# Three masked attention stages rebuilt around 32-row products shared by four heads

## The chip, the cores and the metric

The kernel runs on one core of one Trainium2 chip. The metric is the device time of one execution, in microseconds. The core has a matmul engine (TensorE, PE in the views; its weight loads are PEld), VectorE (DVE), ScalarE (ACT), GpSimd (POOL) and SyncE (SP), which here only issues transfers. The engines run side by side and meet at semaphores.

## The reference

A decoder of four layers works on x of 8 batches, 256 positions and 128 features. Each layer has attention, a second attention (or something like it) and a feed-forward part. The change touches three attention stages, all with 16 heads of 8 features, all computing, for each batch and head,

```python
h = _layernorm(x)
q, k, v = h @ Wq.T + bq, src @ Wk.T + bk, src @ Wv.T + bv   # split in 16 heads of 8
p = softmax(scale * q @ k.T + mask)
x = x + (p @ v) @ Wo.T + bo
```

L0a (layer 0) takes src = h, a causal mask and weights with a rank-32 correction. L0x (layer 0) takes src = the context and the "trinity" mask: 192 image positions see their own third, 64 text positions see all image positions and earlier text. L2a (layer 2) takes src = h, a causal mask and no bias, and turns q and k by rope tables first.

## The kernel before, in words

Weights stay in SBUF, x too (tile x_resid). A prologue (load_and_turn) loads everything by one SP queue, waits for all of it and transposes it on TensorE. The stages follow one another with a barrier between them: L0a, L0x, the layer-0 experts, L1a, L1x, the experts, L2a, L2x, the experts, L3a, L3x, the experts.

A product of 8 features would use 8 of TensorE's 128 rows. The kernel before (multi_head) uses all 128 rows instead: for each head g, VectorE writes kTm[:, g, :], the keys with the 120 rows of the other heads set to zero (L775), and each product contracts 128 rows. Every batch has these steps:

- turn (L591) transposes h; projections (L514, with a 1-row bias product L516 behind each) make q, k and v. keys_and_values (L770 to L775) copies v and k out and makes the 16 masked copies.
- score(g) (L530, L534): for both halves of the queries, q times masked keys with the queries on PSUM's partitions, and the mask as a bf16 product with an identity. VectorE takes each row's maximum (L807). For the 128 first queries only 128 keys are computed.
- The maxima are transposed (L637), negated and split into two bf16 parts, nm (L812, L813).
- logits(g) (L543, L547, L556): the same products with the keys on the partitions, plus the negated maximum by a selecting product, plus the mask. ScalarE takes exp (L721). weigh(g - LAG) (L582) multiplies the probabilities by v, with a column of ones for the sums: six TensorE instructions per head that load 128 columns of weights and stream 9.
- VectorE divides (L834, L836), TensorE transposes y (L670) and projects it (L514, L516), VectorE adds it to x and takes the statistics (L845, L143 to L147).

The order on each engine is written out by hand. In PE's batch loop all 16 scores come first, then the wait for the maxima, then 16 logits with weigh some heads behind, then the next batch's turn and projections and the end of this batch. An f32 product is two instructions in the trace, each with a weight load of its own and each streaming its columns twice; a bf16 product is one.

## Time and profile before

| what | us |
|---|---|
| median of the 2 runs shown (3786.05 to 3790.34) | 3788.2 |
| span of the profiled execution | 3777.7 |
| L0a, from its first h to L0x's first h | 489.22 |
| L0x, to L0n's first h | 494.07 |
| L2a, to L2x's first h | 490.31 |
| PE busy in the whole span | 3163.1 (84%) |

The profiled execution's own time is its span and what lies around it, about 10.5 us by the median. In the views, a time is from the start of the span, "x2" counts instructions, a bracket at a row's end tells how long the engine was idle before and for whom, and PEclk is the granted clock of TensorE: 1.00 is 2.4 GHz and 0.50 is 1.2 GHz. The start of a matmul row is reliable, its end is modelled, so the pace of a stream is read from the distance between starts.

### The profile page before, as it was taken

To read this page: it belongs to the slowest core of one execution; us is meant where nothing else is said; L and a number is where in the kernel's file an instruction comes from. 1 tells how busy PE (TensorE), PEld (TensorE's weight loads), DVE (VectorE), ACT (ScalarE), POOL (GpSimd) and SP (SyncE) were. 2 spreads that over 40 slices of the span, in tenths; PEclk is the share of its full clock that TensorE was granted. 3 is DMA by queue.
4 is the path that set the end of the run, shared out by engine and by line. 5 is a ranking of instruction groups with operands and counts; after the bars stand their busy time and mean duration, and the time that the engine had idled before them with its cause. 6 is when DMAs were issued, how large, how long until landed. Compare 5 with 4: busy or idle time off the path is not lost. (4 is left out here: it accounts for less than half of the span.)

```text
span 3777.7 us, 55936 instructions
## 1 busy us (share of the span) xinstructions
PE 3163.1 (84%) x19172; PEld 2651.0 (70%) x19172; DVE 1363.3 (36%) x4181; ACT 811.9 (21%) x1508; POOL 67.9 (2%) x136
## 2 busy tenths in 40 slices
PE   5999989999769898965896888884699589898699
PEld 4777767777658787843796777673598367676588
DVE  3323232323242535322221333323333354555344
ACT  1111111111122323322232111112233112121222
POOL 1000000000000000000000000000000000000000
PEclk8887878888889899965898889897799589888699
DMA  3000000000000000000002000000000000000000
GB/s 93 0 0 0 0 1 0 0 0 0 1 1 0 0 0 0 0 0 0 0 0 82 1 0 0 0 1 0 1 0 0 0 9 3 6 3 3 1 0 11
DMA packets 19119, 20.41 MB, mean 5 GB/s; under 512 B 1800, under 2 KB 14320, under 8 KB 19056
## 3 DMA queue, kind: packets, MB, share of 16 engines
q1 hardware_dynamic: 19056, 19.59, 1.6%
q8 instruction: 37, 0.61, 0.1%
q14 instruction: 26, 0.21, 0.0%
HBM read 18.54 MB, written 1.05 MB: 5 GB/s over the span
## 5 line engine op out<-in xcount | busy, mean ns | idle before, releaser
L543 PE MATMUL L3x_bank<-L3x_hT,L3x_kTm 128*128 128x256 f32 x512 | 167.3, 424 | 7.6 <-DVE neg_max L813 7.6
L530 PE MATMUL L2a_bank<-L2a_kTm,L2a_qT 128*128 128x128 f32 (+1 forms) x512 | 127.5, 384 | 35.9 <-DVE L2a_kTm L775 24.9
L543 PE MATMUL L2a_bank<-L2a_qT,L2a_kTm 128*128 128x256 f32 (+1 forms) x512 | 150.2, 378 | 7.6 <-DVE neg_max L813 7.6
L543 PE MATMUL L0a_bank<-L0a_qT,L0a_kTm 128*128 128x256 f32 (+1 forms) x512 | 146.9, 372 | 8.9 <-DVE neg_max L813 8.9
L543 PE MATMUL L0x_bank<-L0x_qT,L0x_kTm 128*128 128x256 f32 (+1 forms) x512 | 146.6, 371 | 8.9 <-DVE neg_max L813 8.9
L721 ACT ACTIVATE L3x_probs<-L3x_msum 128x512 f32<-128x512 f32 x128 | 80.6, 630 | 337.9 <-DVE L3x_msum L821 337.9
L565 PE MATMUL L1a_bank<-L1a_qT,L1a_kTm 128*128 128x256 f32 (+1 forms) x512 | 142.4, 360 | 11.5 <-issue 9.7
L821 DVE TENSOR_TENSOR L3x_msum<-L3x_bank,L3x_mcol 128x512 f32<-128x512 f32 x128 | 88.5, 691 | 158.9 <-PE L3x_bank L547 158.2
L721 ACT ACTIVATE L2a_probs<-L2a_bank 128x384 f32<-128x384 f32 x128 | 62.9, 491 | 382.6 <-PE L2a_bank L556 382.6
L1323 PEld LDWEIGHTS L2f_psY<-scores_L_experts_L,L2f_hidden 128*128 128x128 f32 x1024 | 134.1, 193 | 8.9 <-issue 2.6
L1337 PE MATMUL L2f_psG<-hT,scores_L_experts_L 128*128 x512 | 132.3, 384 | 6.5 <-ACTq L42 6.5
L543 PE MATMUL L1a_bank<-L1a_qT,L1a_kTm 128*128 128x256 f32 (+1 forms) x512 | 108.6, 377 | 33.6 <-DVE scores_L_experts_L L784 32.3
L530 PE MATMUL L3x_bank<-L3x_kTm,L3x_hT 128*128 128x256 f32 x512 | 136.1, 423 | 0.0
L1323 PE MATMUL L2f_psY<-scores_L_experts_L,L2f_hidden 128*128 128x128 f32 x1024 | 136.0, 277 | 0.0
L530 PE MATMUL L0x_bank<-L0x_kTm,L0x_qT 128*128 128x128 f32 (+1 forms) x512 | 133.5, 384 | 1.2 <-DVE L0x_kTm L775 1.2
L721 ACT ACTIVATE L0x_probs<-L0x_bank 128x384 f32<-128x384 f32 x128 | 62.9, 491 | 327.2 <-PE L0x_bank L556 327.2
L530 PE MATMUL L0a_bank<-L0a_kTm,L0a_qT 128*128 128x128 f32 (+1 forms) x512 | 131.9, 395 | 1.2 <-DVE L0a_kTm L775 1.2
L721 ACT ACTIVATE L0a_probs<-L0a_bank 128x384 f32<-128x384 f32 x128 | 62.9, 491 | 318.0 <-PE L0a_bank L556 318.0
L582 PEld LDWEIGHTS L3x_psO<-L3x_v,L3x_probs 128*128 128x128 f32 x1024 | 122.5, 192 | 12.3
L543 PEld LDWEIGHTS L1a_bank<-L1a_qT,L1a_kTm 128*128 128x128 f32 x512 | 94.1, 224 | 48.2 <-issue 30.2
L530 PEld LDWEIGHTS L2a_bank<-L2a_kTm,L2a_qT 128*128 128x128 f32 x512 | 85.1, 209 | 58.4 <-DVE L2a_kTm L775 27.3
L1376 DVE SCALAR_TENSOR_TENSOR x_resid<-L2f_psY,L2f_gate,x_resid 128x128 f32 x256 | 78.0, 346 | 132.7 <-PE L2f_psY L1323 130.4
(550 smaller groups left out, 6781.3 us busy)
## 6 DMA issues: line engine op xcount, KB each, us to landing
experts_L_L<-in_L_ffn_w_dram SPq DMA_DIRECT2D x1, 2048.0 KB, 8.2
scores_L_experts_L<-in_L_ffn_w_dram SPq DMA_DIRECT2D x1, 2048.0 KB, 7.8
L3x_mrow<-in_mask_Bx1xSxS_ff_dram SPq DMA_DIRECT2D x8, 256.0 KB, 2.7
experts_L_L<-n_L_ffn_expert_gate_dram SPq DMA_DIRECT2D x1, 1024.0 KB, 13.6
experts_L_L<-in_L_ffn_expert_up_dram SPq DMA_DIRECT2D x1, 1024.0 KB, 7.1
out_dram<-x_resid SPq DMA_DIRECT2D x1, 1024.0 KB
rope_cos_sin<-in_rope_dram SPq DMA_DIRECT2D x1, 256.0 KB
nat_w_attn<-in_L_attn_w_attn_dram SPq DMA_DIRECT2D x1, 192.0 KB
```

The source lines that it names most:

```text
L530: last = nc.tensor.matmul(at, qT[:, t * P:(t + 1) * P], kTm[:, g, 0:KEYS[t]], start=True, stop=not masked, skip_group_check=True)
L543: last = nc.tensor.matmul(at, kTm[:, g, t * P:(t + 1) * P], qT[:, FIRST[t]:S], start=True, stop=stick, skip_group_check=True)
L565: nc.tensor.matmul(at, kTm[:, g, t * P:(t + 1) * P], qT[:, FIRST[t]:S], start=True, stop=False, skip_group_check=True)
L582: last = nc.tensor.matmul(O[:, u, g, :], probs[:, g % RING, q0:q0 + P], v[:, t, g, :], start=j == 0, stop=j == len(tiles) - 1)
L721: nc.scalar.activation(probs[:, g % RING, 0:WIDTH], src[:, 0:WIDTH], ACT.Exp, scale=1.0 if stick else scale).then_inc(s_prob.sem, 1)
L821: nc.vector.tensor_tensor(msum[:, g % RING, :], bank[g % RING][:], mcol[:], ALU.add).then_inc(s_sum.sem, 1)
L1323: last = nc.tensor.matmul(psY[j % 2][:, t * D:(t + 1) * D], hid[:, j % 2, c, t * P:(t + 1) * P], members[j][3][:, c, :], start=c == 0, sto ...
L1337: last = nc.tensor.matmul(bank[u % 2][:, i * S:(i + 1) * S], weight[:, c * P:(c + 1) * P], source[:, bass.ds(b * S, S)], start=True, stop= ...
L1376: last = nc.vector.scalar_tensor_tensor(at, psY[j % 2][:, t * D:(t + 1) * D].unsqueeze(1), gate[:, t, members[j][4]:members[j][4] + 1], at ...
```

## The change

A new function, quad_heads, takes the place of multi_head in L0a, L0x and L2a. L1a and L3x keep multi_head.

- Four heads lie in 32 neighbouring rows. One product contracts these 32 rows and computes four heads side by side: GpSimd makes four copies of k (km) and four of q (qm), copy j keeping head j of every group of four, and a product with 512 columns takes all four. Per turn (four heads) there are three score products (fill) and three logit products (logits) of 512 f32 columns.
- The negated maxima are added by 32-row bf16 products (shift), 512 columns for each of the three logit banks. The masks are added by 128-row bf16 identity products: in fill, 512 columns for each masked block (two of three for the causal mask, all three for trinity), and in hide 1,024 columns per turn for the causal mask and 1,536 for trinity.
- The order is software-pipelined: turn r of batch b computes the logits of batch b and the scores of batch b + 1, weighs the turn before, and carries one piece of the projections of batch b + 2 or of the end of batch b - 1. Loops over batches are unrolled.
- The biases of q and k are added by ScalarE while it copies, from six new one-column loads in the prologue; those of v and the output become one row that GpSimd adds to x. The 1-row bias products of L0a and L0x go, but for one at a stage's start.
- VectorE no longer masks keys; it reduces 512 columns at a time.

In fill, KINDS picks the block of (queries, keys) halves; rows is the group of 32 rows, g = (r + 2) % 4 for fill and r for logits and shift.

On PE, the logits of L0a before: one head (bank is the head's PSUM tile, sel the selecting weights, psO the weighed sums).

```order
L543 MATMUL L0a_bank<-L0a_qT,L0a_kTm 128x256
L547 MATMUL L0a_bank<-neg_max,sel 128x256
L556 MATMUL L0a_bank<-identb,causal 128x128
L543 MATMUL L0a_bank<-L0a_qT,L0a_kTm 128x128
L547 MATMUL L0a_bank<-neg_max,sel 128x128
L556 MATMUL L0a_bank<-identb,causal 128x128
L582 MATMUL L0a_psO<-L0a_v,L0a_probs 128x9 x3
```

And in the changed kernel: one turn of L0a with its four heads, up to the first product of weigh (psS are the banks of the scores, psLA to psLC those of the logits).

```order
L1041 MATMUL L0a_psLA<-L0a_qm,L0a_kT 128x512
L1027 MATMUL L0a_psS<-L0a_km,L0a_qT 128x512
L1031 MATMUL L0a_psS<-causal,identb 128x512
L1041 MATMUL L0a_psLB<-L0a_qm,L0a_kT 128x512
L1051 MATMUL L0a_psLA<-L0a_neg_max,quad_sel 128x256 x2
L1027 MATMUL L0a_psS<-L0a_km,L0a_qT 128x512
L1044 MATMUL L0a_psLC<-L0a_qm,L0a_kT 128x512
L1051 MATMUL L0a_psLB<-L0a_neg_max,quad_sel 128x256 x2
L1027 MATMUL L0a_psS<-L0a_km,L0a_qT 128x512
L1031 MATMUL L0a_psS<-causal,identb 128x512
L1055 MATMUL L0a_psLC<-L0a_neg_max,quad_sel 128x128 x4
L1062 MATMUL L0a_psLA<-identb,causal 128x2x128
```

Scores and logits now alternate, weigh follows in a block of twelve products after the last hide row, and every product of L1027, L1041, L1044, L1051 and L1055 contracts 32 rows, where all rows of the block before contract 128.

On SP's queue in the prologue, the changed kernel has the six columns ahead of the weights:

```order
L261 DMA rope_cos_sin<-in_rope_dram 128x512
L261 DMA w_gate<-in_L_xattn_w_gate_dram 128x1
L261 DMA b_gate<-in_L_xattn_b_gate_dram 128x1
L261 DMA bias_columns<-in_L_attn_b_attn_dram 128x1 x3
L261 DMA bias_columns<-in_L_xattn_bq_dram 128x1
L261 DMA bias_columns<-in_L_xattn_bk_dram 128x1
L261 DMA bias_columns<-in_L_xattn_bv_dram 128x1
L261 DMA nat_L_attn_Wq<-in_L_attn_Wq_dram 128x128
```

The four bias_columns rows are new; all else keeps its order behind them.

The diff, cut to its core (the waits of the helpers left out are those of the semaphores their names tell):

```diff
--- before.py
+++ after.py
...
+BIAS_COLUMNS = {"L0_attn_b_attn": 0, "L0_xattn_bq": 3, "L0_xattn_bk": 4, "L0_xattn_bv": 5}
...
+        loads += [(w["bias_cols"][:, c + j:c + j + 1], dram[n][j * P:(j + 1) * P].rearrange("(p a) -> p a", a=1))
+                  for n, c in BIAS_COLUMNS.items() for j in range(dram[n].shape[0] // P)]
...
+class Hidden:
+
+    near: object
+    cross: object
+    far: object
+    scores: tuple
...
+def quad_heads(nc, mem, w, name, *, wq, wk, wv, wo, wq_rot=None, wk_rot=None, bq=None, bk=None, bv=None, bo=None,
+               cross=False, mask, scale):
+
+    KINDS = ((0, 0), (1, 0), (1, 1))
+    FILLS = 12
...
+                def variants(src, dst, b, used, done):
+                    for sm, value in used:
+                        pool.wait_ge(sm, value)
+                    for j in range(4):
+                        last = nc.gpsimd.tensor_scalar(dst[:, b % 3, j, :], src[:, b % 3, :], w["rows4"][:, j:j + 1], None, ALU.mult)
+                    last.then_inc(done, 1)
...
+                def queries(b):
+                    nc.tensor.matmul(psM[:, 0:S], wq, hT[:, b % 2, :], start=True, stop=True)
+                    if rope:
+                        nc.tensor.matmul(psM[:, S:2 * S], wq_rot, hT[:, b % 2, :], start=True, stop=True).then_inc(s_q, 1)
+                    else:
+                        nc.tensor.matmul(psM[:, S:2 * S], wk, source(b), start=True, stop=True).then_inc(s_q, 1)
...
+                def fill(b, r, k):
+                    i = FILLS * b + 3 * r + k
+                    t, u = KINDS[k]
+                    if i >= 2:
+                        pe.wait_ge(s_red, i - 1)
+                    g = (r + 2) % 4
+                    rows = slice(32 * g, 32 * g + 32)
+                    hidden = mask.scores[k]
+                    last = nc.tensor.matmul(psS[i % 2][:], qT[rows, b % 3, t * P:(t + 1) * P],
+                                            km[rows, b % 3, :, u * P:(u + 1) * P], start=True, stop=hidden is None,
+                                            skip_group_check=True)
+                    if hidden is not None:
+                        last = nc.tensor.matmul(psS[i % 2][:], mem.identb[:], hidden.unsqueeze(1).to_broadcast([P, 4, P]),
+                                                start=False, stop=True, skip_group_check=True)
+                    last.then_inc(s_fill, 1)
+
+                def logits(b, r, k):
+                    i = FILLS * b + 3 * r + k
+                    if i >= 3:
+                        pe.wait_ge(s_prob, i - 2)
+                    rows = slice(32 * r, 32 * r + 32)
+                    if k < 2:
+                        nc.tensor.matmul(psL[k][:], kT[rows, b % 3, 0:P], qm[rows, b % 3, 2 * k:2 * k + 2, :],
+                                         start=True, stop=False, skip_group_check=True)
+                    else:
+                        nc.tensor.matmul(psL[k][:], kT[rows, b % 3, P:S], qm[rows, b % 3, :, P:S],
+                                         start=True, stop=False, skip_group_check=True)
+
+                def shift(b, r, k):
+                    rows = slice(32 * r, 32 * r + 32)
+                    if k < 2:
+                        for a in range(2):
+                            nc.tensor.matmul(psL[k][:, a * S:(a + 1) * S], w["sel4"][rows, 2 * k + a, :], nm[rows, :],
+                                             start=False, stop=False, skip_group_check=True)
+                    else:
+                        for a in range(4):
+                            nc.tensor.matmul(psL[k][:, a * P:(a + 1) * P], w["sel4"][rows, a, :], nm[rows, P:S],
+                                             start=False, stop=False, skip_group_check=True)
+
+                def hide(k):
+                    if k < 2:
+                        at = psL[k][:].rearrange("p (a q) -> p a q", a=2)
+                        two = mem.identb[:].unsqueeze(1).to_broadcast([P, 2, P])
+                        last = nc.tensor.matmul(at[:, :, 0:P], mask.near, two, start=False, stop=True, skip_group_check=True)
+                        if mask.cross is not None:
+                            last = nc.tensor.matmul(at[:, :, P:S], mask.cross, two, start=False, stop=True, skip_group_check=True)
+                    else:
+                        last = nc.tensor.matmul(psL[k][:], mask.far, mem.identb[:].unsqueeze(1).to_broadcast([P, 4, P]),
+                                                start=False, stop=True, skip_group_check=True)
+                    last.then_inc(s_lf, 1)
+
+                def weigh(b, r):
+                    pe.wait_ge(s_prob, FILLS * b + 3 * r + 3)
+                    pe.wait_ge(s_v, b + 1)
+                    if r == 0 and b >= 1:
+                        pe.wait_ge(s_y, b)
+                    for j in range(4):
+                        g = 4 * r + j
+                        first = probs[:, r % 2, j // 2, (j % 2) * S:(j % 2) * S + S]
+                        low = probs[:, r % 2, 2, j * P:(j + 1) * P]
+                        nc.tensor.matmul(O[:, 0, g, :], first[:, 0:P], v[:, b % 3, 0, g, :], start=True, stop=True)
+                        nc.tensor.matmul(O[:, 1, g, :], first[:, P:S], v[:, b % 3, 0, g, :], start=True, stop=False)
+                        last = nc.tensor.matmul(O[:, 1, g, :], low, v[:, b % 3, 1, g, :], start=False, stop=True)
+                    last.then_inc(s_pv, 1)
+
...
+                for b in range(B):
+                    ahead = b + 1 < B
+                    for r in range(4):
+                        if r == 0:
+                            pe.wait_ge(s_qm, b + 1)
+                            if ahead:
+                                pe.wait_ge(s_km, b + 2)
+                        logits(b, r, 0)
+                        if ahead:
+                            fill(b + 1, r, 0)
+                        logits(b, r, 1)
+                        if r == 0:
+                            pe.wait_ge(s_nm, b + 1)
+                        shift(b, r, 0)
+                        if ahead:
+                            fill(b + 1, r, 1)
+                        logits(b, r, 2)
+                        shift(b, r, 1)
+                        if ahead:
+                            fill(b + 1, r, 2)
+                        shift(b, r, 2)
+                        for k in range(3):
+                            hide(k)
+                        if r > 0:
+                            weigh(b, r - 1)
+                        elif b > 0:
+                            weigh(b - 1, 3)
+                        if r == 0 and b + 2 < B:
+                            turn(b + 2)
+                        if r == 1:
+                            if b > 0:
+                                turn_y(b - 1)
+                            if b + 2 < B:
+                                queries(b + 2)
+                        if r == 2:
+                            if b > 0:
+                                project(b - 1)
+                            if b + 2 < B and rope:
+                                keys(b + 2)
+                        if r == 3:
+                            if b + 2 < B:
+                                values(b + 2)
+                            if ahead:
+                                turn_max(b + 1)
+                weigh(B - 1, 3)
+                turn_y(B - 1)
+                project(B - 1)
...
+                            act.wait_ge(s_lf, i + 1)
+                            if 4 * b + r >= 2:
+                                act.wait_ge(s_pv, 4 * b + r - 1)
+                            nc.scalar.activation(probs[:, r % 2, k, :], psL[k][:], ACT.Exp, scale=scale).then_inc(s_prob, 1)
...
+                def reduce(b, r, k):
+                    i = FILLS * b + 3 * r + k
+                    g = (r + 2) % 4
+                    dve.wait_ge(s_fill, i + 1)
+                    if k == 0:
+                        if b >= 1 and r == 0:
+                            dve.wait_ge(s_mxt, b)
+                        dst = mx[:, 0, g, 0:4]
+                    else:
+                        dst = part[:, k - 1, g, :]
+                    at = psS[i % 2][:].rearrange("p (j n) -> p j n", j=4)
+                    nc.vector.tensor_reduce(dst, at, AX.X, ALU.max).then_inc(s_red, 1)
+
+                def gather_max(b):
+                    dve.wait_ge(s_red, FILLS * (b + 1))
+                    steps.step(nc.vector.tensor_tensor(mx[:, 1, :, 0:4], part[:, 0, :, :], part[:, 1, :, :], ALU.max))
+                    nc.vector.tensor_copy(mx[:, :, :, 4:8], mx[:, :, :, 0:4]).then_inc(s_mx, 1)
+
...
-        causal = [[(w["causal"][:], 0, P)], [(w["causal"][:], P, S)]]
-        trinity = [[(w["trinity"][:, 0, 0:P], 0, P)], [(w["trinity"][:, 1, :], 0, S)]]
+        at, tb = w["causal"][:], w["trinity"]
+        causal = Hidden(at, None, at, (at, None, at))
+        trinity = Hidden(tb[:, 0, 0:P], tb[:, 1, 0:P], tb[:, 1, P:S], (tb[:, 0, 0:P], tb[:, 1, 0:P], tb[:, 1, P:S]))
...
-        multi_head(nc, mem, w, "L0a", wq=W0[:, 0:P], wk=W0[:, P:2 * P], wv=W0[:, 2 * P:3 * P], wo=w["L0_attn_w_proj"][:],
+        quad_heads(nc, mem, w, "L0a", wq=W0[:, 0:P], wk=W0[:, P:2 * P], wv=W0[:, 2 * P:3 * P], wo=w["L0_attn_w_proj"][:],
                    bq=0, bk=1, bv=2, bo=3, mask=causal, scale=qk)
-        multi_head(nc, mem, w, "L0x", wq=w["L0_xattn_Wq"][:], wk=w["L0_xattn_Wk"][:], wv=w["L0_xattn_Wv"][:],
-                   wo=w["L0_xattn_Wo"][:], bq=4, bk=5, bv=6, bo=7, cross=True, mask=trinity, scale=qk)
+        quad_heads(nc, mem, w, "L0x", wq=w["L0_xattn_Wq"][:], wk=w["L0_xattn_Wk"][:], wv=w["L0_xattn_Wv"][:],
+                   wo=w["L0_xattn_Wo"][:], bq=3, bk=4, bv=5, bo=7, cross=True, mask=trinity, scale=qk)
...
-        multi_head(nc, mem, w, "L2a", wq=w["L2_attn_Wq"][:], wq_rot=w["L2_attn_Wq_rot"][:], wk=w["L2_attn_Wk"][:],
+        quad_heads(nc, mem, w, "L2a", wq=w["L2_attn_Wq"][:], wq_rot=w["L2_attn_Wq_rot"][:], wk=w["L2_attn_Wk"][:],
                    wk_rot=w["L2_attn_Wk_rot"][:], wv=w["L2_attn_Wv"][:], wo=w["L2_attn_Wo"][:], mask=causal, scale=qk)
```

## Rows read from the trace of the kernel before

**Rows 1.** The page's slices: granted TensorE clock in tenths, 40 slices of the span.

```profile
PEclk8887878888889899965898889897799589888699
```

**Rows 2.** Stretches of L0a, L0x, L2a: window, length, busy time by engine, clock, DMA.

```profile
43.55:532.77 489.22, 452.65 (x2800) 361.34 (x2800) 149.93 (x497) 74.89 (x157) 0.59 (x2) 0.84 0.00 0
532.77:1026.84 494.07, 458.88 (x2928) 366.69 (x2928) 150.32 (x496) 74.30 (x156) 2.95 (x8) 0.85 0.00 0
2068.07:2558.38 490.31, 416.87 (x2736) 348.36 (x2736) 161.98 (x520) 71.37 (x149) 0.00 (x0) 0.88 0.00 0
```

**Rows 3.** Timeline of PE in L0a's logits: start, us, engine, line, tiles, form.

```profile
153.13 0.79 PE L582 MATMUL L0a_psO<-L0a_v,L0a_probs 128*128 128x9 f32 x6
153.77 0.68 PE L543 MATMUL L0a_bank<-L0a_qT,L0a_kTm 128*128 128x256 f32 x2
154.29 0.27 PE L547 MATMUL L0a_bank<-neg_max,sel 128*128 128x256 bf16 x1
154.40 0.22 PE L556 MATMUL L0a_bank<-identb,causal 128*128 128x128 bf16 x1
```

**Rows 4.** Timeline of PE in L2a's first projections.

```profile
2071.51 1.06 PE L514 MATMUL L2a_psK<-L2a_hT,wT_L_attn_Wk 128*128 128x256 f32 x2
2072.36 1.06 PE L514 MATMUL L2a_psQ<-L2a_hT,wT_L_q_rot 128*128 128x256 f32 x2
```

**Rows 5.** Timeline of PE in L0a's projections, with 1-row bias products.

```profile
104.70 1.22 PE L514 MATMUL L0a_psK<-L0a_hT,wT_L_attn 128*128 128x256 f32 x2
105.85 1.22 PE L516 MATMUL L0a_psK<-ones_row,bias_rows 1*128 1x256 f32 x2
107.00 0.80 PE L514 MATMUL L0a_psT<-wT_L_attn,L0a_hT 128*128 128x128 f32 x2
```

**Rows 6.** Timeline of PE in L1x's output projection, at clock 1.00.

```profile
1661.52 0.46 PE L1013 MATMUL L1x_psY<-wT_L_xattn_Wh,L1x_yT 128*128 128x128 f32 x2 [0.55 <-ACT L1x_yT L1070]
1661.91 0.48 PE L1014 MATMUL L1x_psY<-bias_rows,ones_row 1*128 1x128 f32 x2
```

**Rows 7.** Timeline of PE at the end of L0a's first batch.

```profile
97.73 3.63 PE L582 MATMUL L0a_psO<-L0a_v,L0a_probs 128*128 128x9 f32 x24
```

**Rows 8.** Stretches by clock: L0a, L2x, and L0a again, columns as Rows 2.

```profile
102.43:109.89 7.46, 7.46 (x16) 3.96 (x16) 0.00 (x0) 0.00 (x0) 0.00 (x0) 0.50 0.00 0
2560.70:2564.50 3.80, 2.90 (x8) 2.25 (x9) 0.42 (x1) 0.65 (x2) 0.00 (x0) 0.58 0.00 0
120.00:131.00 11.00, 11.00 (x77) 9.05 (x75) 7.76 (x26) 0.00 (x0) 0.00 (x0) 1.00 0.00 0
98.00:99.50 1.50, 1.50 (x15) 1.50 (x15) 0.00 (x0) 0.42 (x1) 0.00 (x0) 1.00 0.00 0
99.50:101.20 1.70, 1.70 (x10) 1.70 (x10) 0.00 (x0) 0.00 (x0) 0.00 (x0) 0.50 0.00 0
```

**Rows 9.** Timeline of PE in the prologue: the only 32-row products.

```profile
35.47 0.88 PE L330 MATMUL lora<-lbT_attn,nat_la_attn 32*128 32x384 f32 x2 [0.47 <-DVE wT_L_up L354]
36.19 0.38 PE L331 MATMUL lora<-lbT_proj,nat_la_proj 32*128 32x128 f32 x2
```

**Rows 10.** Timeline of the prologue: one column load's issue, and PE's first product.

```profile
11.19 0.60 SPq L254 DMA_DIRECT2D bgq<-in_L_xattn_bgq_dram  x1
27.27 0.87 PE L326 MATMUL turn<-ident,nat_w_attn 128*128 128x128 f32 x3 [27.27 <-DMA bias_rows<-in_L_xattn_wo_b_dram]
```

**Rows 11.** Groups by line, engine and form: busy us, mean ns, idle before.

```profile
L494 POOL COPY L0x_cT<-ctx_T 128x256 f32 x8 | 3.2, 401 | 371.2 <-PE L0x_psT L516 370.8 <-PEq L42 0.4
L821 DVE TENSOR_TENSOR L3x_msum<-L3x_bank,L3x_mcol 128x512 f32<-128x512 f32 x128 | 88.5, 691 | 158.9 <-PE L3x_bank L547 158.2 <-ACT L3x_probs L721 0.8
L721 ACT ACTIVATE L3x_probs<-L3x_msum 128x512 f32<-128x512 f32 x128 | 80.6, 630 | 337.9 <-DVE L3x_msum L821 337.9
```

**Rows 12.** L0a before its first score and after its last weigh, columns as Rows 2.

```profile
43.55:54.56 11.01, 8.19 (x18) 4.28 (x18) 2.01 (x6) 1.46 (x3) 0.00 (x0) 0.50 0.00 0
521.03:532.77 11.74, 3.34 (x10) 2.19 (x10) 2.33 (x9) 2.77 (x5) 0.59 (x2) 0.57 0.00 1
```

More of the change, by code:

```diff
@@ L11 @@
 from contextlib import ExitStack
+from dataclasses import dataclass
 import numpy as np
@@ L200, in load_and_turn @@
         lora_done, chain = sem("lora_done"), sem("prologue_chain")
+        lanes = sem("lanes")
+        lane, kind = sb("lane", [P, P], I32), sb("lane_kind", [P, 3, P], I32)
+        slot = sb("lane_slot", [P, 2, P])
         turns = [(w_attn[:, j, :], w["L0_attn_w_attn"][:, j * P:(j + 1) * P]) for j in range(3)]
@@ L261, in _ @@
                 steps = Chain(pool, Count(built, 0))
+                nc.gpsimd.iota(lane[:], pattern=[[0, P]], base=0, channel_multiplier=1).then_inc(lanes, 1)
                 for dst in (mem.ident, mem.identb):
@@ L1600, in decoder @@
         w["rows"] = sb("head_rows", [P, H])
+        w["rows4"], w["low4"], w["sel4"] = sb("quad_rows", [P, 4]), sb("low_rows", [P, 1]), sb("quad_sel", [P, 4, P], BF16)
+        w["bias_cols"] = sb("bias_columns", [P, 6])
         w["neg_tri"], w["neg_ones"], w["ones"], w["earlier"] = (sb(n, [P, P]) for n in ("neg_tri", "neg_ones", "ones", "earlier"))
```

281 lines of the change are left out of this document (added).

## The prediction

> **What bounds the kernel now.** I read the page's slices first, then stretches of the three stages, PE's timeline inside them, and last the granted clock against what PE was doing. The slices show a clock that moves between its two levels all along [rows 1]. In the stages PE is busy for 452.65 of 489.22 us (L0a), 458.88 of 494.07 (L0x) and 416.87 of 490.31 (L2a), with VectorE below 162 us and ScalarE below 75 [rows 2]: PE is the bound, at a mean clock of 0.84 to 0.88. The three last 1473.6 us together. So two things decide: how many columns PE streams, and at which clock.
>
> **Prices at 1.2 GHz.** Two f32 instructions of 256 columns start 0.85 us apart from the next two [rows 4]: 3.33 ns per f32 column. A bf16 column passes once where an f32 column passes four times over its two instructions (0.11 us for 256 bf16 columns beside 0.52 for 256 f32 ones at full clock [rows 3]), so 0.83 ns. At 2.4 GHz all is half. Six weigh instructions take 0.64 us at full clock [rows 3], 0.107 each; of the 24 from 97.73 to 101.21 the part after 99.5 runs at 0.50 [rows 7, 8]: 1.77 us at 0.107 make 16.5 of them, so the other 7.5 take 1.71 us, 0.23 each. I take 0.213, twice 0.107.
>
> **A turn, causal.** A turn stands for four heads. f32: six products of 512 columns, 3,072 columns. bf16: two masks in fill (1,024), shift (1,536), hide (1,024), 3,584 columns. At 1.2 GHz 10.24 + 2.99 = 13.2 us. Weigh stays 24 instructions, 5.1 us. Trinity has 1,024 bf16 columns more, 14.1 us.
>
> **Changes between 32 and 128 rows.** The trace has them with 1-row products: 128-row and 1-row f32 pairs follow each other 1.15 us apart where the columns take 0.85 [rows 5], so 0.30 us at 1.2 GHz; at full clock 0.39 where two instructions of 128 columns take 0.22 [rows 6], near 0.2. For bf16 products, with one weight load, I take 0.2 at 1.2 GHz, between nothing and 0.30. A causal turn has six changes, two into f32, so 2 x 0.3 + 4 x 0.2 = 1.4 us; a trinity turn eight, 1.9 us. A turn is then 19.7 us (causal) or 21.1 (trinity), if nothing overlaps.
>
> **Two row groups at once.** No row shows it: the only 32-row products share one row group [rows 9] and run at the pace of their columns (0.72 us from L330 to L331 for a pair of 384 columns, which by the price at 2.4 GHz is 0.64). logits and fill use different row groups, so the last instruction of one may run beside the first of the next: bounds nothing, and 2.1 us in a causal turn (0.85 for L1041/L1027, 0.85 for L1027/L1044, two halves of a shift) or 1.3 in a trinity turn, where a 128-row mask stands in between. I take half, since no row is nearer to one end. The page "TensorE: Matmul & The Clock Gate" of the Trainium skill, Part 3 (packing small matmuls), measured 3.07 times the pace for four row tiles and says that products in different row groups start some 4 ns apart; by it the full saving would be taken, 88 us less than my sum; no run here shows it.
>
> **The rest of a stage.** Between turns PE keeps turn, queries, values, turn_max, turn_y and project: in L0a and L0x 1,024 f32 columns (3.4 us at 1.2 GHz) and 768 columns of transposes with one instruction each instead of two (1.3 us), 4.7 us a batch; in L2a 512 f32 columns more, 6.4 us. Times 8: 38 and 51 us. The 1-row bias products, kTm's wait and the idle stretch before each batch's logits go; they are in the 1473.6 that I subtract. Head and tail: L0a has 11.01 us before its first score with PE idle for 2.8, and 11.74 after its last weigh with PE idle for 8.4 [rows 12]; the new head adds four GpSimd copies and the turn of the maxima with nothing beside it, so I take 18 us of idle a stage.
>
> **What costs nothing.** GpSimd's eight masked copies per batch: 0.40 us for a copy of that size [rows 11], 3.2 us, even at three times that 10 us, beside 80 us of PE's work; without that cover PE would wait at each batch's first turn. VectorE's three reductions of 512 columns, by a 512-column operation from PSUM 0.69 us each, and ScalarE's three exps at 0.63 [rows 11] lie beside a turn of 20 us. shift's first wait is for the maxima, which VectorE negates while PE does the two logits and one fill ahead of it; behind it on PE stands the whole turn, so a late maximum would delay everything by its own length, 1 to 2 us a batch, and I leave that to the upper end. The prologue gains six column loads on SP ahead of the weights, 0.6 us each and a gap (a 64-row one takes 0.60 to issue), and PE's first product waits for SP's last load at 27.27 [rows 10]: +3.8 us. VectorE's new small operations run while x is loading.
>
> **The sum.** L0a 32 x 19.7 + 38 + 18 = 686; L0x 32 x 21.1 + 38 + 18 = 731; L2a 630 + 51 + 18 = 699. Together 2116, less 1473.6 makes +642, +4 for the prologue: +646. Less half of the overlap (67 + 42 + 67 = 176): +558. The profiled execution's 3777.7 us of span become 4336, and with the 10.5 us around the span **4346 us**, against 3788.2 (+15%). All of this holds if PE runs at 1.2 GHz through the three stages, which is what has to be argued.
>
> **Why the clock should stay low.** What did PE do when the clock moved? It rose within 3.8 us of L2x's full-row f32 projections, with PE busy for only 2.90 (mean 0.58 [rows 8]). It stayed at 0.50 through 7.46 us of L0a's projections, in which PE was busy all the time, but half of it with 1-row products [rows 8, 5]. It stays at 1.00 through scores whose masked keys are zero in 120 of 128 rows [rows 8], the stretch from 120 to 131: the values don't count, the rows of the instruction do. And it falls at 99.5 with PE busy all the time, in products that stream 9 columns [rows 7, 8]. So being busy is not enough; what holds the clock is columns streamed through many rows. In the new turn of 19.7 us, full rows stream 2,048 bf16 columns (1.7 us, 9%); even with each 32-row product counted as a quarter (11.5 us, 2.9) it is 4.6 us, 23%, and at full clock the shares are about the same. L0a's projections, at half, didn't rise. The projections of a batch come in pieces of at most 2.6 us with 32-row or weigh products on both sides, so they should not lift it either, or for a moment.
>
> **Rivals.** (1) *The clock stays high: faster.* If a 32-row product counts as a full one, PE streams without gaps and the clock holds at 1.00. For it: PE has fewer idle times, and the 32-row products of the prologue ran at the pace of 2.4 GHz [rows 9], though for under 2 us, which is too short to tell. Against: the 1-row stretch. Price: causal turns 6.6 + 2.6 + 0.95 = 10.15 us, trinity 10.9, the pieces 19, 19 and 26 us a stage, idle 18: 362 + 386 + 369 = 1117 us, so -357, +4, and half of an overlap of 88: -397, or **3391 us**. It decides as soon as turns are left at 1.00 for more than a few us at a time. The page "TensorE: Matmul & The Clock Gate" of the Trainium skill, Part 1, ties the clock to how busy the PE has been and asks only for matmuls without gaps; by that rule this rival is the forecast and the change is worth 10%. The trace disagrees in the 7.46 busy us at 0.50 [rows 8].
>
> (2) *The clock moves.* The mask products and projections lift it in each batch and a part of the turns runs at 1.00. PE's work of some 2060 us at 1.2 GHz loses half of what falls in these stretches: a quarter of it at full clock gives 4090 us, a half 3830, two thirds about 3660. For it: the old stages do move, and trinity has the most 128-row columns. Against: the share of 23% above is the same in every turn.
>
> (3) *The columns bind even less than I think*: complete overlap and free changes of rows at 1.2 GHz. The 151 us of changes (45 + 61 + 45) and the other 88 us of overlap go: 4346 - 239 = **4107 us**. This is the low end of my own case, its high end no overlap (+88) and 1 us of waiting in each of the 96 turns: 4530.
>
> **Chances and numbers.** The forecast's case (1.2 GHz, 4107 to 4530) has 0.77; the moving clock 0.10, spread over 3660 to 4090; the high clock 0.13. The range 4030 to 4530 takes in the first case and the slower part of the second, 0.80 in all. Within 2% (76 us, about what a measurement can tell from no change) lie only the better outcomes of the moving clock, 0.03; faster is the high clock and its neighbourhood, 0.14; slower 0.83.
>
> **What the profile after would show.** The clock of the three stages: 0.50 to 0.55 by the forecast, over 0.9 by rival 1. The distance from one L1041 (first bank) to the next: near 19 us in L0a, 20.5 in L0x, with PE busy throughout; 10 with the high clock. L1041 and the following L1027 less than 1.7 us apart would show overlap. A wait of PE on the negated maxima or on GpSimd's copies would show a cover that I thought safe to be missing. The forecast is wrong if 32-row products keep the clock up; then everything after that step turns round in sign.

## The result, and the profile after

The changed kernel takes **3920.2 us** (median of 2 runs, 3917.9 to 3922.5) against 3788.2: a ratio of 1.037 with a 95% interval from 1.034 to 1.040. I had forecast 4346, between 4030 and 4530. The sign is right and the size is not: +132 us where I said +558, and 110 us under the low end. Between the two profiled spans the difference is 143 us (3920.8 for 3777.7), and the sums below are of spans. The profiled execution took 3922.5 us, 1.7 more than its span; the 10.5 us that I had put around a span were mostly the difference between one execution of the kernel before and another.

The granted clock in the page's slices, to be laid beside [rows 1]:

```profile
PEclk7555555555559999875699555556699679898699
```

And the stretches of L0a, L0x and L2a, from each stage's first h to the next stage's, with the columns of [rows 2]:

```profile
46.40:575.00 528.60, 514.11 (x1717) 308.12 (x1717) 103.53 (x216) 66.25 (x134) 64.54 (x74) 0.51 0.00 1
575.00:1136.91 561.91, 548.44 (x1812) 312.32 (x1812) 103.59 (x216) 65.14 (x133) 63.46 (x72) 0.51 0.00 0
2182.45:2693.30 510.85, 496.04 (x1744) 298.88 (x1744) 115.86 (x233) 58.62 (x117) 69.50 (x80) 0.54 0.00 0
```

The clock went where I said, to 0.51 to 0.54 from 0.84 to 0.88. The stages take 1601.4 us against 1473.6 [rows 2]: +39, +68 and +21, together +127.8 (differences of the rows above and [rows 2]). The start of L0a comes 2.9 us later (46.40 for 43.55). The unchanged stages give the rest: 1136.91 to 2182.45 is 4.3 us longer than 1026.84 to 2068.07 was, and what follows 2693.30 is 8.2 us longer than what followed 2558.38. These 12.5 us need not come from the change: the runs of the kernel before in experiment 12 lie between 3767.6 and 3795.4.

Now one turn of L0a, in the timeline of PE (start, us, engine, line, tiles, form). Its program order is logits LA, fill, mask, logits LB, shift LA, fill, logits LC, shift LB, fill, mask:

```profile
309.45 1.22 PE L1041 MATMUL L0a_psLA<-L0a_qm,L0a_kT 32*128 32x512 f32 x1
309.45 1.22 PE L1027 MATMUL L0a_psS<-L0a_km,L0a_qT 32*128 32x512 f32 x1
310.46 1.06 PE L1041 MATMUL L0a_psLA<-L0a_qm,L0a_kT 32*128 32x512 f32 x1
310.47 1.06 PE L1027 MATMUL L0a_psS<-L0a_km,L0a_qT 32*128 32x512 f32 x1
311.46 0.61 PE L1031 MATMUL L0a_psS<-causal,identb 128*128 128x512 bf16 x1
311.99 1.22 PE L1041 MATMUL L0a_psLB<-L0a_qm,L0a_kT 32*128 32x512 f32 x1
312.01 1.22 PE L1027 MATMUL L0a_psS<-L0a_km,L0a_qT 32*128 32x512 f32 x1
...
313.86 0.63 PE L1051 MATMUL L0a_psLA<-L0a_neg_max,quad_sel 32*128 32x256 bf16 x2
314.29 1.06 PE L1044 MATMUL L0a_psLC<-L0a_qm,L0a_kT 32*128 32x512 f32 x1
314.29 1.22 PE L1027 MATMUL L0a_psS<-L0a_km,L0a_qT 32*128 32x512 f32 x1
...
316.00 0.63 PE L1051 MATMUL L0a_psLB<-L0a_neg_max,quad_sel 32*128 32x256 bf16 x2
...
318.46 0.44 PE L1079 MATMUL L0a_psO<-L0a_v,L0a_probs 128*128 128x9 f32 x2
...
323.44 1.20 PE L1016 MATMUL L0a_psN<-wT_L_attn,L0a_hT 128*128 128x128 f32 x4
```

Two things are to be seen. A logits product and a fill run side by side **as whole pairs**: both first instructions start at 309.45, both second ones at 310.46 and 310.47, and 2.01 us after the start (311.46) both products are through. And the fill at 312.01 **has overtaken the shift** that stands ahead of it in the program and starts only at 313.86; the fill at 314.29 overtakes the other one (316.00). So each of the three logits products of a turn has a fill beside it. In L0x it is the same: in one of its turns the pairs start at 860.03, 862.57 and 865.54, with at most 0.02 us between the two. From 309.45 to weigh at 318.46 are 9.0 us, weigh takes 5.0 more.

### The profile page after: what moved, and what is told of

It reads as the page before. It is cut to its first block and busy times, and to the rows that moved or that the text cites. A ratio compares the mean times of both kernels' runs of the same rounds, so it can differ in the third digit from the quotient of the medians.

```text
span 3920.8 us, 46486 instructions
## 1 busy us (share of the span) xinstructions
PE 3406.5 (87%) x15980; PEld 2506.8 (64%) x15980; DVE 1226.7 (31%) x3347; ACT 781.4 (20%) x1430; POOL 263.2 (7%) x356
## 5 line engine op out<-in xcount | busy, mean ns | idle before, releaser
L1027 PE MATMUL L0a_psS<-L0a_km,L0a_qT 32*128 32x512 f32 x192 | 195.6, 1123 | 1.4 <-POOL L0a_km L948 1.4
L1027 PE MATMUL L0x_psS<-L0x_km,L0x_qT 32*128 32x512 f32 x192 | 194.5, 1113 | 1.4 <-POOL L0x_km L948 1.4
L1027 PE MATMUL L2a_psS<-L2a_km,L2a_qT 32*128 32x512 f32 x192 | 182.6, 1052 | 0.1
L584 PE MATMUL L1a_bank<-L1a_qT,L1a_kTm 128*128 128x256 f32 (+1 forms) x512 | 142.4, 360 | 11.5 <-issue 9.7
L562 PE MATMUL L1a_bank<-L1a_qT,L1a_kTm 128*128 128x256 f32 (+1 forms) x512 | 109.5, 379 | 31.7 <-DVE scores_L_experts_L L803 30.2
L1821 PE MATMUL L1f_psG<-hT,experts_L_L 128*128 x512 | 124.2, 387 | 2.2 <-ACTq L43 2.1
L586 PE MATMUL L1a_bank<-L1a_softplus,neg_tri 128*128 128x256 f32 (+1 forms) x512 | 125.6, 327 | 0.0
L601 PE MATMUL L3x_psO<-L3x_v,L3x_probs 128*128 128x9 f32 x1024 | 125.4, 253 | 0.0
L1807 PEld LDWEIGHTS L1f_psY<-experts_L_L,L1f_hidden 128*128 128x128 f32 x1024 | 123.1, 192 | 2.9
L549 PEld LDWEIGHTS L3x_bank<-L3x_kTm,L3x_hT 128*128 128x128 f32 x512 | 105.7, 215 | 28.8 <-issue 9.6
L1807 PE MATMUL L1f_psY<-experts_L_L,L1f_hidden 128*128 128x128 f32 x1024 | 123.4, 275 | 0.0
L821 DVE CUSTOM_DVE_ANT_0 L3x_junk<-L3x_bank,L3x_mrow 128x256 f32<-128x256 f32 x256 | 98.6, 422 | 44.2 <-PE L3x_bank L549 22.0
```

Source lines behind the costliest of these rows:

```text
L549: last = nc.tensor.matmul(at, qT[:, t * P:(t + 1) * P], kTm[:, g, 0:KEYS[t]], start=True, stop=not masked, skip_group_check=True)
L562: last = nc.tensor.matmul(at, kTm[:, g, t * P:(t + 1) * P], qT[:, FIRST[t]:S], start=True, stop=stick, skip_group_check=True)
L584: nc.tensor.matmul(at, kTm[:, g, t * P:(t + 1) * P], qT[:, FIRST[t]:S], start=True, stop=False, skip_group_check=True)
L586: last = nc.tensor.matmul(at, w["neg_tri"][:], soft[:, g, AT[t]:AT[t] + n], start=False, stop=False, skip_group_check=True)
L601: last = nc.tensor.matmul(O[:, u, g, :], probs[:, g % RING, q0:q0 + P], v[:, t, g, :], start=j == 0, stop=j == len(tiles) - 1)
L821: last = nc.vector.tensor_tensor_reduce(out=junk[:, t, :], in0=bank[g % RING][:, t * S:(t + 1) * S], in1=mrow[:, t, :], scale=1.0, scalar= ...
```

## Experiments

Experiments 1 to 11 are one run each, with the kernel before at 3781.5 to 3784.4 us beside them; experiment 12 has four runs.

**1. No second row group.** Fills and reductions take the row group of the logits:

```
-                    g = (r + 2) % 4
+                    g = r
```

> Fills and reductions take the same row group as the logits of the turn (r in place of r + 2), so that no two row groups are in use side by side; everything else, the result too, stays. Theory A (the forecast missed because whole pairs of f32 products in two row groups run side by side): at 309 us of the changed kernel a logits and a fill together take 2.01 us up to the mask, one after the other they would take 4 x 0.85 and a change of rows, 3.5. Three such pairs a turn, in 28 turns of a stage: 1.5 x 3 x 84 = 380 us. It gives 4300 us (4250 to 4350), with L1041 and the following L1027 1.7 us apart and a turn of 18 to 19 us. Rival B (the columns, the changes of rows or the weigh products cost less than I priced, and the overlap little): at most the 2.1 us a turn that I had as the upper bound, of it the half, about 90 us: under 4100. The clock stays at 0.50 by both.

Measured: 4376.2 us. Its three stages (columns of [rows 2]), and the start of a turn in its timeline:

```profile
46.40:718.40 672.00, 657.42 (x1717) 355.32 (x1717) 103.57 (x216) 66.28 (x134) 64.54 (x74) 0.51 0.00 0
718.40:1429.50 711.10, 697.59 (x1812) 363.18 (x1812) 103.58 (x216) 65.18 (x133) 63.48 (x72) 0.50 0.00 0
2472.70:3150.50 677.80, 663.26 (x1744) 360.91 (x1744) 114.70 (x232) 58.35 (x117) 69.43 (x80) 0.51 0.00 0
```

```profile
325.06 2.07 PE L1041 MATMUL L0a_psLA<-L0a_qm,L0a_kT 32*128 32x512 f32 x2
326.93 1.91 PE L1027 MATMUL L0a_psS<-L0a_km,L0a_qT 32*128 32x512 f32 x2
328.77 0.61 PE L1031 MATMUL L0a_psS<-causal,identb 128*128 128x512 bf16 x1
329.30 2.07 PE L1041 MATMUL L0a_psLB<-L0a_qm,L0a_kT 32*128 32x512 f32 x2
331.17 0.63 PE L1051 MATMUL L0a_psLA<-L0a_neg_max,quad_sel 32*128 32x256 bf16 x2
331.60 1.91 PE L1027 MATMUL L0a_psS<-L0a_km,L0a_qT 32*128 32x512 f32 x2
...
339.18 0.43 PE L1079 MATMUL L0a_psO<-L0a_v,L0a_probs 128*128 128x9 f32 x2
```

The same two products now take 3.71 us (325.06 to 328.77) in place of 2.01, and the way to weigh 14.12 in place of 9.01. The shift (331.17) now runs ahead of the fill (331.60), as in the program. The 5.11 us come in 84 turns (28 a stage have fills): 429 of the 459.5 us by which the stages grew (2060.9 for 1601.4); most of the rest is in L2a, where the clock is 0.51 and was 0.54. Rival B is out. The time is 76 us over my 4300 and 26 over my range: 49 of the 76 are that I had put 3.5 us for what takes 3.71 (380 us for 429), and most of the rest is L2a's.

**2. All rows.** The f32 products of logits and fill contract 128 rows:

```
-                    rows = slice(32 * g, 32 * g + 32)
+                    rows = slice(0, P)
```

> The f32 products of logits and fill contract all 128 rows in place of 32 (the scores are then sums over four heads and wrong); columns, order, masks, shifts and weigh products stay. Theory A (the clock of the three stages is low because 32-row products do not hold it): the same columns with all rows lift it. At full clock a turn is 6 x 0.85 + 1.5 + 2.6 = 9.2 us, at 1.2 GHz 18.4; with the clock at 0.75 to 1.0, as in the kernel before, the three stages take 1050 to 1350 us in place of the 1600 of the changed kernel, and the whole 3350 to 3650 us, although nothing runs side by side any more. Rival C (the clock is low for another reason: the weigh products, the masks or the missing idle time): it stays at 0.50, and with the overlap gone the time rises to about 4300 us.

Measured: 3512.4 us; the stages:

```profile
46.30:428.80 382.50, 369.52 (x1717) 208.09 (x1717) 103.59 (x216) 66.30 (x134) 64.46 (x74) 0.93 0.00 1
428.80:835.60 406.80, 394.75 (x1812) 222.69 (x1812) 103.67 (x217) 65.16 (x133) 63.41 (x72) 0.90 0.00 1
1879.30:2288.30 409.00, 394.32 (x1744) 222.98 (x1744) 115.67 (x232) 58.40 (x117) 69.48 (x80) 0.88 0.00 1
```

The same number of instructions (x1717, x1812, x1744) with the same columns: the clock is at 0.88 to 0.93 and 1198 us stand for 1601, although nothing overlaps. With the rows the overlap goes too, but experiment 1 is without overlap and stays at 0.50 to 0.51, so the rows make this difference; rival C is out.

**3. The kernel before with 32 rows.**

```
-  nc.tensor.matmul(at, qT[:, t * P:(t + 1) * P], kTm[:, g, 0:KEYS[t]],
+  nc.tensor.matmul(at, qT[0:32, t * P:(t + 1) * P], kTm[0:32, g, 0:KEYS[t]],
```

> The kernel before, with the f32 products of scores and logits in its three stages (L530, L543) cut to rows 0 to 31, in one row group, columns and order unchanged (the heads of the other rows get zero scores). Theory A: rows alone turn the clock off: granted clock of the three stages from 0.84 to 0.88 down to 0.50 to 0.55. A head at 1.2 GHz: 768 f32 columns 2.56 us, some 900 bf16 columns 0.75, six weigh products 1.28, changes of rows 0.5, together 5.1 x 128 and 50 for the rest is 700 us a stage in place of 490: 4400 us (4250 to 4600). Rival C: rows do not matter for the clock, the time stays at 3790 or falls a little.

Measured: 5077.8 us. L0a's stretch, and two of its logits products of 256 and 128 columns:

```profile
45.20:963.40 918.20, 881.68 (x2800) 538.20 (x2800) 150.77 (x496) 74.75 (x157) 0.54 (x2) 0.50 0.00 0
```

```profile
441.43 1.22 PE L544 MATMUL L0a_bank<-L0a_qT,L0a_kTm 32*128 32x256 f32 x2
442.58 0.39 PE L548 MATMUL L0a_bank<-neg_max,sel 128*128 128x256 bf16 x1
442.77 0.32 PE L557 MATMUL L0a_bank<-identb,causal 128*128 128x128 bf16 x1
443.01 0.79 PE L544 MATMUL L0a_bank<-L0a_qT,L0a_kTm 32*128 32x128 f32 x2
443.74 0.29 PE L548 MATMUL L0a_bank<-neg_max,sel 128*128 128x128 bf16 x1
```

The clock falls from 0.84 [rows 2] to 0.50, as said. The size I missed (918 us for 700): a product takes 1.15 us where 256 columns take 0.85 [rows 4], and 0.73 for 128, 0.30 each for the change of rows, the price of [rows 5]; a head has four, and I had put 0.5 us for all its changes. A head takes 6.1 us in all (2.31 for its scores, from 80.19 to 82.50, and 3.82 for logits and weigh, from 447.87 to 451.69) for my 5.1, and the rest of the stage some 135 for my 50.

**4. A push at the start of each stage**, to see whether the low clock is a second state of the same kernel:

```
                 turn_max(0)
+                warm(64)        # bf16, 128 rows, 224 columns, into psO[:, 288:512]
                 for b in range(B):
```

(The push was put behind turn_max, ahead of the first turn, not at the place that the expectation tells.)

> The changed kernel with 64 bf16 products of 224 columns over all 128 rows, into unused columns of psO, at the head of each of the three stages, right after PE's wait for the first masked keys and before the first fills (their product is not used; the result stays). 64 x 224 columns are 12 us at 1.2 GHz and 6 at full clock. Theory A: the clock rises during them and falls again within the first fills and turns, since these do not hold it: 3920 + 3 x 8 = 3945 us (3930 to 3960), stages' clock 0.50 to 0.55. Rival D (the low clock is a state that feeds itself: once up, the faster turns with two row groups side by side would hold it): the clock stays up for long stretches, a turn is then 7 us in place of 14, and the time falls below 3700, at best to 3200.

Measured: 3888.7 us. The push, the turns after it, and what follows:

```profile
82.34:90.18 7.84, 7.84 (x66) 6.96 (x64) 1.13 (x3) 0.00 (x0) 0.00 (x0) 0.79 0.00 0
90.18:102.70 12.52, 12.38 (x75) 6.83 (x75) 4.15 (x6) 3.42 (x7) 0.00 (x0) 1.00 0.01 1
102.70:140.00 37.30, 36.69 (x121) 21.02 (x121) 7.52 (x15) 3.99 (x8) 7.91 (x9) 0.50 0.00 1
```

Two turns, the first without a weigh, ran at full clock; at the end of the first weigh it fell. The time is 31 us under the changed kernel (one run), not 25 over it as by theory A, so the brief rises seem to outweigh the pushes. Theory A holds in the main, rival D's long stretches did not come, and the first weigh, whose products stream 9 columns, became the suspect.

**5 to 8. Full-row products in weigh, or weigh spread out.** warm(n) is n such products, whose result nobody reads:

```
                 for j in range(4):
+                    warm(3)        # with and without the push; warm(1) in a third kernel
                     g = 4 * r + j
```

> The kernel with 64 full-row products at each stage's head, and besides three bf16 products of 224 columns over 128 rows (unused columns of psO) ahead of each head in weigh, 12 a turn; the result stays. In the kernel with the head alone the clock stood at 1.00 through the first turns and fell inside the first weigh, at 102.7 us; such a turn took 4.8 us to its weigh and 2.6 in it. Theory A (rows streamed hold the clock, and weigh is where they lack): the clock stays at 1.00; a turn is 4.8 + 2.6 + 12 x 0.1 = 8.6 us with 0.6 for the projections, a stage 32 x 9.2 and 25 for head and tail, 320 us in place of 534: 3920 - 3 x 214 = 3280 us (3180 to 3400). Rival C (weigh turns the clock off for what it is, many short products or weight loads, not for lack of streamed rows): clock 0.50 again and 3920 + 96 x 2.4 = about 4150 us, the extra products at 0.2 us each.

> The same 12 extra products a turn, without the 64 at the stage's head; the result stays. Rival D (the low clock feeds itself: at 1.2 GHz a turn streams its rows over twice the time): with a turn of 14 + 2.4 us the share of time with full rows streaming is too small, the clock does not rise by itself or late, and the time is 4000 to 4150 us. Theory A without such a second state: the extra products in weigh lift the clock in the first turns, and it comes out as with the head, near 3280.

> 64 full-row products at the head, no others; weigh's 24 products of a turn are spread over it: six behind the first fill, six behind the third, twelve at the end; the result stays. Theory A, if what counts is how long PE goes without streaming rows: the longest such stretch is halved from 2.6 to 1.3 us at full clock and the clock stays up for many turns where before it fell in the first weigh: L0a under 450 us, total 3250 to 3700. Rival: the mean of a turn decides, not where in it weigh stands: it falls within a few turns as with the head alone, 3880 to 3920 us.

> As the kernel with the head and 12 extra products a turn, but with one ahead of each head in weigh, 4 a turn; the result stays. If 4 are enough, the clock is 1.00 and the time about 96 x 0.8 = 75 us under that of 12 (near 3200); if not, the clock falls in some weigh and does not come back in the stage, and the time is between 3300 and 3950 us.

Measured: 4024.7 us with three and the push, 4083.4 with three without it, 3943.8 with one and the push; with weigh in three pieces 3915.8. None held the clock. With three and the push, in L0a:

```profile
85.20:122.80 37.60, 37.15 (x271) 25.28 (x269) 8.93 (x15) 7.40 (x15) 7.92 (x9) 1.00 0.00 1
122.80:400.00 277.20, 275.20 (x1047) 171.39 (x1048) 51.39 (x108) 31.55 (x64) 31.69 (x36) 0.50 0.00 1
```

```profile
101.29 0.45 PE L1110 MATMUL L0a_psO<-trinity,identb 128*128 128x224 bf16 x3
101.58 0.30 PE L1080 MATMUL L0a_psO<-L0a_v,L0a_probs 128*128 128x9 f32 x2
```

The clock stood at 1.00 until 122.80, with the push alone until 102.70, and then fell all the same, behind a weigh that took from 118.26 to 121.81. My 3180 to 3400 was wrong, and so it might have been the weigh products as such (rival C, with about 4150). But three products in a row cost 0.29 us of weigh's time (101.29 to 101.58), and the six weigh instructions behind them ran bare. With weigh in three pieces (six instructions behind the first fill, six behind the third, twelve at the end) and no products added, the clock fell between 102 and 103 us, as with the push alone: shorter bare stretches by themselves did not hold it, and more full rows in threes did not either.

**9 and 10. One between any two products of weigh**, with the push and without:

```
+                    warm(1)
                     nc.tensor.matmul(O[:, 0, g, :], first[:, 0:P], ...)
+                    warm(1)
                     nc.tensor.matmul(O[:, 1, g, :], first[:, P:S], ...)
+                    warm(1)
                     last = nc.tensor.matmul(O[:, 1, g, :], low, ...)
```

> 64 full-row products at each stage's head, and one bf16 product of 224 columns over 128 rows between any two products of weigh, 12 a turn, as in the kernel with three ahead of each head, only spread between the weight loads; the result stays. In that kernel the clock stood at 1.00 for 37 us, three turns, and then fell; three such products in a row cost 0.29 us and the six weigh instructions behind them have none beside them; in the kernel with one ahead of each head at 1.2 GHz the product is hidden beside the weight load (a head of weigh starts 1.305 us after the last, where six instructions take 1.28). Theory A (rows streamed per time hold the clock): weigh now streams 224 columns in each 0.23 us where it streamed 672 in 0.93, a third more per time, and the clock holds at 1.00 through the stages; a turn 4.8 + 2.8 + 0.6 us, a stage 300 to 360 us: 3920 - 1600 + 1000 = 3320 us (3230 to 3420). Rival C (weigh turns the clock off for its many weight loads): 24 more loads in it, and it falls in the first turns: 3950 to 4050 us.

> The same with one product at each stage's head in place of 64; the result stays. Rival D, by now part of theory A (there are two states, since at 1.2 GHz the same rows are spread over twice the time): the clock does not rise in the turns, 3930 to 4000 us, the extra products being nearly hidden. If the turns themselves lift the clock, it comes out as with the 64, about 3320 us.

Measured: **3398.6 us** with the push. L0a up to its last batch and from there to its end, and a piece of weigh:

```profile
87.20:333.00 245.80, 242.23 (x1835) 158.67 (x1833) 86.08 (x177) 53.51 (x108) 47.44 (x54) 1.00 0.00 1
333.00:398.30 65.30, 58.18 (x258) 41.58 (x256) 3.93 (x15) 10.07 (x18) 1.07 (x2) 0.50 0.00 1
```

```profile
311.43 0.26 PE L1112 MATMUL L0a_psO<-trinity,identb 128*128 128x224 bf16 x1
311.52 0.30 PE L1080 MATMUL L0a_psO<-L0a_v,L0a_probs 128*128 128x9 f32 x2
311.68 0.26 PE L1112 MATMUL L0a_psO<-trinity,identb 128*128 128x224 bf16 x1
```

The clock is at 1.00 for 246 us on end, in L0x from 440 to 700 and in L2a from 1870 to 2110 likewise, with 12 extra products a turn as in experiment 5, but between the weight loads. A weigh product and its companion take 0.25 us (311.43 to 311.68), where the two weigh instructions alone take 0.21 [rows 3]: 224 columns streamed for 0.04. Inside a stage it falls only in the last batch, where no fills are left. Rival C is out: weigh has as many weight loads as in experiment 5, 36 a turn for the 24 of the changed kernel, and the clock holds. Without the push it was 3596.3, and there I had both cases wrong: the clock stayed at 0.50 for 262.8 us of L0a and then rose in the turns:

```profile
42.50:305.30 262.80, 252.73 (x933) 143.45 (x933) 56.65 (x116) 32.83 (x66) 40.70 (x47) 0.50 0.00 1
305.40:428.20 122.80, 121.11 (x916) 79.08 (x916) 44.60 (x95) 26.43 (x53) 23.72 (x27) 1.00 0.00 1
```

So there are two states of one and the same sequence, either lasting, and something rare passes it from one to the other. In all three stages the rise came right behind the pair of full-row projections in the second turn of a batch (L993 at 303.55 in L0a, 698.82 in L0x, 2105.75 in L2a). The batches before had the same pair without a rise; why it came there stays open.

**11. What the masks cost.**

```
-                    hidden = mask.scores[k]
+                    hidden = None
...
-                        for k in range(3):
-                            hide(k)
```

> The changed kernel without the mask products of fill and hide (all keys count, so the result is not the reference's). It prices what the masks cost on TensorE: in a causal turn two masks of fill, 0.54 us each from start to the next start, and hide's three, 0.83 us, 1.9 us; in a trinity turn three and 1.25, 2.9 us; at 1.2 GHz 32 x (1.9 + 2.9 + 1.9) = 214 us: 3705 us (3670 to 3760), clock 0.50. If only the columns counted and the changes of rows were free, it would be 0.43 a mask: 0.43 x 2 + 0.83 and 0.43 x 3 + 1.25, 187 us. Either would say that the change without masks on TensorE would still be within 2 to 3% of the kernel before.

Measured: 3672.4 us; the stages are 456.40, 456.80 and 446.70 us long, 241 us less than the changed kernel's. The mask products thus cost more in it than all its loss of 132 us. But they are not what the change added: the kernel before has them on TensorE too, with as many columns (65,536 in L0a, by L534 and L556 before and by L1031, L1062 and L1066 after). So the 3% by which this run lies under the kernel before is no fair comparison; what that one would gain without its masks was not tried.

**12. The last batch.** One product of 512 columns behind each logits product there, and 40 in place of 64 in the push:

```
                         logits(b, r, 0)
+                        if not ahead:
+                            warm_scores()
```

> The kernel with one full-row product between any two products of weigh, with 40 in place of 64 at each stage's head, and in the last batch of a stage, where no fills go along, one product of 512 columns over 128 rows (into a bank of the scores that is free by then) behind each of the three logits products; the result stays. Without these the clock stood at 1.00 from 87 us to the last batch (333.0 us) in L0a and fell there. Theory A: it now holds to the stage's end; the last four turns and the end go from some 13 us each to 7.5, some 20 us a stage, and 24 products less at each head are 2 us more: 3399 - 3 x 22 = 3333 us (3310 to 3400), about 0.88 of the kernel before and 0.85 of the changed kernel. If 40 products do not lift the clock in one of the stages, that stage stays at 1.2 GHz and the time is 3550 or more; if the three products are too little for the last batch, it is 3390 to 3410.

Measured: 3414.6 us (four runs, 3410.3 to 3418.8), a ratio of 0.903 to the kernel before (0.900 to 0.906). 40 products are enough for the push in all three stages. The last batch was not won, in none of them:

```profile
331.40:402.00 70.60, 63.48 (x265) 40.35 (x264) 4.03 (x15) 10.13 (x18) 1.07 (x2) 0.50 0.00 0
```

The clock fell at 331.4, in the last batch's first turn, and at 1.2 GHz the new products cost about 12 x 0.43 = 5 us a stage, 15 in all, which is about the difference to experiment 9. Why the last batch does not hold the clock is open. That one's 3398.6 is one run only; the sure statement is that such a version is 9.7% under the kernel before and, by 3414.6 to 3920.2 on another chip, some 13% under the change as it was made.

## Why the prediction was right and where it was wrong

**The clock: right.** The step on which the sign hung was that 32-row products don't hold the clock. The stages ran at 0.51 to 0.54; experiments 2 and 3 turn it on and off by the rows, in both kernels, with PE busy in all of them. The page "TensorE: Matmul & The Clock Gate" of the Trainium skill, Part 1, which ties the clock to how busy PE is and which stood behind my first rival, is not borne out here: PE was busy for 514 of 528.6 us of L0a at 0.51.

**The step that failed: "Two row groups at once".** I let only the last instruction of one product run beside the first of the next in program order, at most 2.1 us in a causal turn and 1.3 in a trinity turn, and took half: 88 us in all. Experiment 1 measures 5.11 us in a causal turn, 5.3 in a trinity turn (149.2 us in 28 turns of L0x), and 459.5 us for the three stages. Two assumptions were wrong: that the two instructions of one product can't run beside both of the other, and that a product can't pass one that is queued ahead of it in another row group. I had called the 2.1 a bound where no row bore it out; the honest upper bound was three full fills a turn, 3 x 1.71 = 5.1 us, and that is what came. (I had also let it count in 32 turns, where 28 have fills.) This is also why rival 3, my low end of 4107, was 187 us too high: it stood on the same bound. Part 3 of the same page of the Trainium skill has products in different row groups start about 4 ns apart and four row tiles run at 3.07 times the pace, and I read that into my narrow frame. The trace agrees with the first (the first instructions of a pair are 0.00 to 0.02 us apart); with two groups the pace here is 3.71 / 2.01 = 1.85 times. Part 2 (step-by-step) of the same page of the Trainium skill says that the matmuls themselves stay in program order and only weight loads are pulled ahead; the trace disagrees, by the fill at 312.01 and the shift at 313.86.

**The other terms** are tested by experiment 1, which is my sum without overlap: 2060.9 us against 686 + 731 + 699 = 2116, 2.6% less. A causal turn up to weigh was to take 10.24 + 2.99 + 1.4 = 14.6 us and takes 14.12: the changes of rows are smaller. A mask takes 0.53 us up to the next 32-row product (311.46 to 311.99) where its columns take 0.43, so 0.10 for a change that I had at 0.2; an f32 product after a change takes 1.87 us in place of 1.71, 0.16 for my 0.3. Weigh was 5.1 by forecast and is 5.0 (318.46 to 323.44).

The account: 4336 - 3920.8 = 415 us too much. Overlap 459.5 - 88 = 371.5; the other terms 2116 - 2060.9 = 55; the prologue 1 (2.9 for 4); less 12.5 in the unchanged stages, which I had at nothing. The other 11 us to 4346 less 3920 are the 10.5 around the span.

**What I had at nothing.** GpSimd's masked copies take twice the 0.40 us that I read from a plain copy [rows 11], and are hidden all the same, but for PE's wait at the stage's start:

```profile
51.76 3.89 POOL L948 TENSOR_SCALAR L0a_km<-L0a_kT,quad_rows 128x256 f32<-128x256 f32 x4 [5.51 <-ACT L0a_kT L1191]
55.70 1.12 PE L1027 MATMUL L0a_psS<-L0a_km,L0a_qT 32*128 32x512 f32 x2 [1.44 <-POOL L0a_km L948]
```

PE did not wait on the negated maxima in the turns; the 1 us a turn of my high end was not needed.

**Rivals.** The high clock, rival 1 (3391 us), did not come by itself, and yet its number was near what experiment 9 reaches (3398.6): the state exists, it only has to be entered and fed. That the two numbers are so close is chance: experiment 9 has extra products and stretches at 0.50 that the rival had not, and the whole overlap where it had half of 88 us. Rival 2 gave the moving clock 3660 to 4090, and 3920 lies in it, but for another reason.

## What to carry to other kernels

Before a change cuts the rows of TensorE's products, ask what then holds the clock: PE can be busy all the time at 1.2 GHz. Where products of different row groups follow each other, count them as side by side, whole, even past products queued between them, with full-row products as the limit: none was seen to be passed here. And products that nobody reads can pay: 64 in a push at the start of a stage and one between any two weight-bound products, where 224 columns cost 0.04 us, took some 520 us off the changed kernel (3920.2 to 3398.6, one run on another chip).

## What the runs showed of the hardware

- Of two f32 products in two row groups all four instructions interleave: 2.01 us for both at 1.2 GHz, 1.06 at 2.4 (in experiment 9, from 306.61 to 307.67), against 3.71 one after the other. A product overtakes one of another row group that is ahead of it in the program (312.01 against 313.86); in one row group the order is kept (experiment 1).
- The same instructions and columns run at a clock of 0.50 to 0.54 with 32 rows, with overlap or without, and at 0.88 to 0.93 with 128, PE being busy for 96 to 98% of the stage in all.
- The same sequence stays at either clock: at 0.50 for 262.8 us and then at 1.00 without a push (experiment 10), at 1.00 for 245.8 us after one (experiment 9).
- Twelve full-row products a turn in threes did not hold the clock (experiment 5), the same twelve one by one between weight loads did (experiment 9).
- A GpSimd product with a column of scalars, 128x256 f32, takes 0.90 to 0.97 us, a copy of that size 0.40.
